# Gate-up product of the experts: 384-column steps that meet the rows' high and low part at once, and a 128-row down product

## What is computed

```python
# x: 4096 tokens x 512; CAP = 192 slots per expert, TOP_K = 8, INTER = 192
xb  = rows of x that each expert got                      # (48, 192, 512)
gu  = jnp.einsum('ech,eoh->eco', xb, gate_up_proj)        # (48, 192, 384)
g, u = jnp.split(gu, 2, axis=-1)
h   = jax.nn.silu(g) * u                                  # (48, 192, 192)
out = jnp.einsum('eci,ehi->ech', h, down_proj)            # (48, 192, 512)
final = zeros.at[tok].add(y * w[:, None])                 # y: rows of out, w: routing weights
```

## Time and profile before

| | |
|---|---|
| median of 3 runs | 1123.43 us (1120.83 to 1123.87) |
| the profiled execution | 1120.8 us |
| its span, first to last instruction | 1119.1 us |
| mean granted TensorE clock | 0.963 |
| busy: TensorE, weight loads | 1040.8 us (93%), 820.0 us (73%) |
| busy: VectorE, ScalarE, GpSimd | 872.7 (78%), 626.7 (56%), 551.8 us (49%) |
| chain that ended last | DMA 25%, TensorE 25%, issue 19%, GpSimd 13%, VectorE 11% |

### The profile page before, as it was taken

One profiled execution on the slowest core, in us unless ns is written; L12 is line 12 of the kernel. 1 busy time (PEld: TensorE's weight loads), 2 busy tenths in 40 slices (PEclk: granted clock), 3 DMA queues, 4 the chain that ended last, 5 costly groups with the idle time before them and its releaser, 6 DMA issues.

```text
span 1119.1 us, 24715 instructions
## 1 busy us (share of the span) xinstructions
PE 1040.8 (93%) x6474; PEld 820.0 (73%) x6474; DVE 872.7 (78%) x2429; ACT 626.7 (56%) x1751; POOL 551.8 (49%) x529
## 2 busy tenths in 40 slices
PE   5998999999999999999999963899999999999992
PEld 4776778878787787878878742777777787778771
DVE  5776888888888888889888753478787787877771
ACT  4554455454555545555455531567676677676761
POOL 2114666666666566666666646124343333333333
PEclk9999999999999999999999975699999999999996
DMA  7999565535231131211212110489999999999973
GB/s 295 364 289 291 201 246 175 183 138 178 72 101 48 47 94 47 92 49 59 82 47 86 39 48 23 147 237 257 242 257 239 250 248 251 244 255 243 255 172 46
DMA packets 94050, 185.70 MB, mean 166 GB/s; under 512 B 24791, under 2 KB 24791, under 8 KB 93504
## 3 DMA queue, kind: packets, MB, share of 16 engines
q1 hardware_dynamic: 62640, 145.10, 40.3%
q0 software_dynamic: 31376, 40.20, 16.5%
HBM read 116.00 MB, written 122.00 MB: 213 GB/s over the span
## 4 chain that ended last, share of the span: by engine, by line
DMA 25%; PE 25%; issue 19%; POOL 13%; DVE 11%; ACT 3%; POOLq 1%; DVEq 1%; SPq 0%; ACTq 0%
DMA layer_out<-qk_both,scatter_idx 21%; PE ps L1180 11%; POOL slot_records L541 6%; PE ps L1165 5%; POOL layer_out L622 4%; DVE qk_both L998 3%; POOL rstd L552 3%; PE ps L1170 2%; PE ps L1298 2%; DMA x_ln<-in_x 2%; DVE diff L993 1%; PE ps L1319 1%; PE ps L1202 1%; DMA slot_records<-row,slot_idx 1%; DMA w_raw<-slot_records 1%
## 5 line engine op out<-in xcount | busy, mean ns | idle before, releaser
L541 POOL DMA_INDIRECT slot_records<-row,slot_idx x256 | 266.4, 1041 | 89.7 <-issue 59.6
L622 POOL DMA_INDIRECT layer_out<-qk_both,scatter_idx x96 | 143.5, 1495 | 262.3 <-DVE scatter_idx L1099 206.2
L552 POOL TENSOR_TENSOR rstd<-mv,neg_half 128x1 f32<-128x1 f32 x96 | 80.2, 835 | 130.4 <-DVE mv L911 78.8
L1180 PE MATMUL ps<-w_high,xn_high 128*128 128x512 f32 x384 | 114.0, 419 | 0.7 <-ACT xn_high L637 0.7
L672 ACT ACTIVATE probs<-ps,neg_max_s 128x128 f32<-128x128 f32 x256 | 89.9, 377 | 33.2 <-DVE neg_max_s L908 33.2
L1180 PE MATMUL ps<-w_low,xn_high 128*128 128x512 f32 x384 | 107.8, 403 | 0.0
L1180 PE MATMUL ps<-w_high,xn_low 128*128 128x512 f32 x384 | 107.0, 401 | 0.0
L637 ACT ACTIVATE xn_t<-ps 128x512 f32<-128x512 f32 x64 | 38.3, 599 | 117.4 <-PE ps L1165 117.4
L1319 PE MATMUL ps<-w_high 128*128 128x192 f32 x576 | 94.1, 286 | 3.6 <-DVE w_low L1085 3.3
L1319 PE MATMUL ps<-w_low,w_high 128*128 128x192 f32 x576 | 89.8, 279 | 0.0
L1319 PE MATMUL ps<-w_high,w_low 128*128 128x192 f32 x576 | 89.6, 278 | 0.0
(11 more groups left out here) (162 smaller groups left out, 2407.6 us busy)
## 6 DMA issues: line engine op xcount, KB each, us to landing
gu_sb<-in_gate_up SPq DMA_DIRECT2D x48, 768.0 KB, 5.4
slot_records<-dn_both SPq DMA_DIRECT2D x6, 3366.0 KB, 23.0
w_raw<-slot_records SPq DMA_DIRECT2D x48, 280.5 KB, 4.7
dn_both<-in_down_proj SPq DMA_DIRECT2D x48, 256.0 KB
x_ln<-in_x SPq DMA_DIRECT2D x32, 256.0 KB
x_res<-in_x SPq DMA_DIRECT2D x32, 256.0 KB, 3.0
ctx_t_sb<-in_ctx_t SPq DMA_DIRECT2D x32, 256.0 KB
ctx_sb<-in_ctx_rows SPq DMA_DIRECT2D x32, 256.0 KB
```

The source lines that it names most:

```text
L541: pool.indirect_dma_start(out=records, out_offset=bass.IndirectOffsetOnAxis(ap=slot_idx[:, s.parity, k:k + 1], axis=0), in_=row[:, s.parit ...
L552: pool.tensor_tensor(rstd[:, :], mv[:, 1:2], neg_half[:, 0:1], ALU.pow).then_inc(steps.sem, 1)
L622: pool.indirect_dma_start(out=out, out_offset=bass.IndirectOffsetOnAxis(ap=scatter_idx[0:PART[h], d.parity, h:h + 1], axis=0), in_=y[0:PAR ...
L1180: last = pe.matmul(dst, left[:, c, :], right[:, m, c, :], start=(n == 0 and c == 0), stop=(n == 2 and c == KC - 1))
```

## The change

The parts of the rows come to lie beside each other (`rows_both`, 2 x 192 columns), and a step of the gate-up product with the weights' high part takes both, 384 columns, into one bank: columns 0 to 191 collect high x high, columns 192 to 383 high x low. The 4 steps with the weights' low part add low x high to the second half. A block now has 8 matmuls instead of 12 and fills its own bank (2, 3 and 6). The two halves are added outside TensorE: ScalarE copies the second half to SBUF (`gu_part`: blocks 0 and 1 in one copy, block 2 in another), VectorE adds the first half to it (`gu_sum`: one addition for blocks 0 and 1, two for block 2, which bring the up part from partitions 64 to 127 down to 0 to 63), and silu and the products h1 and h2 read `gu_sum`. `gu_part` and `gu_sum` lie over the attention's `v_sb` and `probs`.

In the down product the last step takes all 128 rows of `h2_rest`, whose upper half is set to zero once, in place of 64.

```diff
@@ split_buffers
-        gu_high, rows_high, dn_high, dn2_both, h1_high, h2_twice = split_buffers(w_high)
-        gu_low, rows_low, dn_low, _, h1_low, h2_rest = split_buffers(w_low)
+        gu_high, rows_both, dn_high, dn2_both = split_buffers(
+            w_high, (2, KC, 2 * INTER), (2, KC, 2 * CAP), (2, 1, DM), (2, 1, DM))
...
+        rows_high, rows_low = rows_both[:, :, :, 0:CAP], rows_both[:, :, :, CAP:2 * CAP]
@@ ScalarE, expert_turn
                     act.wait_ge(gup_t.sem, gup_t.after(u, "first"))
                     if u.back(1).exists():
-                        act.wait_ge(gup_v.sem, gup_v.after(u.back(1), "h2"))
-                    act.activation(silu1[:, :], ps[:, 2, 0:CAP], ACT.Silu).then_inc(gup_a.sem, 1)
+                        act.wait_ge(gup_v.sem, gup_v.after(u.back(1), "sum2"))
+                    copy(gu_part[:, 0:2, :], ps[:, 2:4, CAP:2 * CAP], gup_a)
                     act.wait_ge(gup_t.sem, gup_t.after(u, "second"))
-                    act.activation(silu2[:, :], ps[0:INTER - P, 3, 0:CAP], ACT.Silu).then_inc(gup_a.sem, 1)
+                    copy(gu_part[:, 2, :], ps[:, 6, CAP:2 * CAP], gup_a)
+                    act.wait_ge(gup_v.sem, gup_v.after(u, "sum1"))
+                    act.activation(silu1[:, :], gu_sum[:, 0, :], ACT.Silu).then_inc(gup_a.sem, 1)
+                    act.wait_ge(gup_v.sem, gup_v.after(u, "sum2"))
+                    act.activation(silu2[:, :], gu_sum[0:INTER - P, 2, :], ACT.Silu).then_inc(gup_a.sem, 1)
@@ VectorE, expert_turn
                 if u.exists():
+                    dve.wait_ge(gup_a.sem, gup_a.after(u, "part1"))
+                    if u.back(1).exists():
+                        dve.wait_ge(gup_v.sem, gup_v.after(u.back(1), "h2"))
+                        dve.wait_ge(gup_a.sem, gup_a.after(u.back(1), "silu2"))
+                    dve.tensor_tensor(gu_sum[:, 0:2, :], ps[:, 2:4, 0:CAP], gu_part[:, 0:2, :], ALU.add)\
+                        .then_inc(gup_v.sem, 1)
+                    dve.wait_ge(gup_a.sem, gup_a.after(u, "part2"))
+                    dve.tensor_tensor(gu_sum[0:INTER - P, 2, :], ps[0:INTER - P, 6, 0:CAP], gu_part[0:INTER - P, 2, :],
+                                      ALU.add)
+                    dve.tensor_tensor(gu_sum[0:INTER - P, 3, :], ps[INTER - P:P, 6, 0:CAP], gu_part[INTER - P:P, 2, :],
+                                      ALU.add).then_inc(gup_v.sem, 1)
...
-                    dve.tensor_tensor(h1[:, :], silu1[:, :], ps[:, 2, CAP:2 * CAP], ALU.mult).then_inc(gup_v.sem, 1)
+                    dve.tensor_tensor(h1[:, :], silu1[:, :], gu_sum[:, 1, :], ALU.mult).then_inc(gup_v.sem, 1)
                     dve.wait_ge(gup_a.sem, gup_a.after(u, "silu2"))
-                    dve.tensor_tensor(h2[:, :], silu2[:, :], ps[INTER - P:P, 3, 0:CAP], ALU.mult)\
+                    dve.tensor_tensor(h2[:, :], silu2[:, :], gu_sum[0:INTER - P, 3, :], ALU.mult)\
...
+                    if u.first():
+                        dve.memset(h2_rest[INTER - P:P].bitcast(FP32), 0.0)
@@ TensorE, expert_turn
                     if u.back(1).exists():
-                        pe.wait_ge(gup_v.sem, gup_v.after(u.back(1), "h2"))
+                        pe.wait_ge(gup_v.sem, gup_v.after(u.back(1), "sum2"))
...
-                        pairs = [(gu_high, rows_high), (gu_high, rows_low), (gu_low, rows_high)]
-                        for n, (left, right) in enumerate(pairs):
-                            for k in range(KC):
-                                last = pe.matmul(dst, left[:, u.parity, k, cols], right[:, u.parity, k, :],
-                                                 start=(n == 0 and k == 0), stop=(n == 2 and k == KC - 1))
+                        for k in range(KC):
+                            pe.matmul(bank[:, 0:2 * CAP], gu_high[:, u.parity, k, cols], rows_both[:, u.parity, k, :],
+                                      start=(k == 0), stop=False)
+                        for k in range(KC):
+                            last = pe.matmul(bank[:, CAP:2 * CAP], gu_low[:, u.parity, k, cols],
+                                             rows_high[:, u.parity, k, :], start=False, stop=(k == KC - 1))
...
-                                 (h2_twice, dn2_both, P), (h2_low, dn2_both, INTER - P)]
+                                 (h2_twice, dn2_both, P), (h2_rest, dn2_both, P)]
```

More of the change, by code:

```diff
@@ L310, in decoder_layer @@
         gup_t = Steps(sem("gate_up_tensor"), "first second")
-        gup_a = Steps(sem("gate_up_scalar"), "silu1 silu2 high1 high2 again")
-        gup_v = Steps(sem("gate_up_vector"), "h1 h2 low1 low2")
+        gup_a = Steps(sem("gate_up_scalar"), "part1 part2 silu1 silu2 high1 high2 again")
+        gup_v = Steps(sem("gate_up_vector"), "sum1 sum2 h1 h2 low1 low2")
         wgu_a = Steps(sem("gate_up_weights_scalar"), "high")
```

18 lines of the change are left out of this document (11 added, 7 removed).

## The result

| | before | changed |
|---|---|---|
| median | 1123.65 us (4 runs, 1120.83 to 1124.88) | 1141.30 us (4 runs, 1140.45 to 1143.16) |
| the profiled execution, its span | 1120.8, 1119.1 us | 1143.16, 1141.4 us |
| one turn of the loop, mean of 43 | 8.09 us | 8.59 us |

The changed kernel takes 1.0154 times as long, 95% interval 1.0116 to 1.0192: slower by 17.6 us. The forecast was slower by 5.6, at 1129; 1141.3 lies near the upper end of its range. The sign and the mechanism held; a part of the mechanism was sized far too small.

A forecast was written before the change was run, and what follows sets the result against it. Three loops near 8 us bound the expert stage; the lengthened ring makes the period 8.30: 43 turns +8.6, first turns 0, end -1.5, together +7, so 1128, and 1129 us against the runs' median. Range 1114 to 1143.

The forecast's parts named there:

- Three loops near 8 us: Expert stage: TensorE's work, the scatter-adds, and a ring of ScalarE and VectorE all close at nearly 8 us.
- the scatters' loop: GpSimd issues an expert's two scatter-adds only after the previous expert's have landed; claimed 8.0 to 8.1 us beside the loads.
- TensorE's turn 8.0 to 6.9: TensorE's work per expert falls from 8.0 to about 6.9 us: 0.6 saved in gate-up, 0.5 in the down product.
- The gaps of 0.32 and 0.43: Down product: start distances around its 64-row step, 0.75 us together; as a 128-row step it saves 0.29.
- ScalarE's copies cost nothing: ScalarE's two copies out of PSUM are covered by VectorE's gu_low (1.76 us); without that cover up to 0.87 per turn.
- The ring at 8.17: Loop from gu_low through index, sums, silu2 and ScalarE's copies to the next gu_high, lengthened from about 6.8 to 8.17 us.
- The lower end: Ring 0.23 us shorter if the gaps at two joints around the third sum and h1 are absent.
- The index's wait ... I take 0.13, near the lower end.: VectorE's index waiting for a scatter landing adds 0 to 0.4 us per turn, taken as 0.13: period 8.30.
- First turns 0, tail -1.5: Half-clock first turns: TensorE's gain cancels the added sums, 0; the end: scatters hang less far behind, -1.5 us.
- Faster: Rival: the ring does not close, so TensorE's gain shows; at best 1107 us, chance 0.14.
- No change, the scatters set the pace: Rival: scatters set the pace as before, or the shorter end pays; 0 to +3 us, 1121 to 1126, chance 0.22.
- Clock: Rival: TensorE's pauses of about 1.2 us lower its clock in the loop; +4.2 us per such turn, chance 0.03.

The follow-up runs named there:

- experiment 11: Kernel before, with SyncE starting the next gate-up load at the end of VectorE's turn, down weights and rows behind it: 1118.5 us, ratio 0.9962.
- experiment 9: Changed kernel, with SyncE starting the next gate-up load at the end of VectorE's turn, down weights and rows behind it: 1128.5 us, ratio 1.0053.
- experiment 5: Changed kernel without ScalarE's two part copies and VectorE's three sums, TensorE's work kept as changed: 1125.3 us, ratio 1.0006.
- experiment 1: Changed kernel, with VectorE making the scatter index just before y1 instead of between gu_low and the sums: 1133.6 us, ratio 1.0084.

## Why the prediction was right in direction and short in size

- **Three loops near 8 us.** Right, and the most useful part. What I missed is that the scatters' loop was closed in nearly every turn: before, the scatters follow each landing by a steady 1.5 us. The chain of waits by line says it in one row (64.8% in the scatters' DMA), and I had read it only for its first turns. TensorE's loop is close behind: in the new order (experiment 11) most turns are its 8.00 and 8.03.
- **TensorE's turn 8.0 to 6.9.** Right: 0.18 and 0.11 us per step, 85% busy in a turn of 8.6 is 7.3, part of it at a lower clock; in experiment 9, at full clock, 85% of 8.24 is 7.0. The gaps of 0.32 and 0.43 are gone. Worth nothing in the loop, as forecast (experiment 5). The Trainium skill's figure for the step, 163 ns from "TensorE: Matmul & The Clock Gate", section Back-to-back issue gap, was a little low: 0.73 / 4 = 0.18 was measured.
- **ScalarE's copies cost nothing.** Right: 848.59 to 849.66, under gu_low, and ScalarE then sits idle 2.48 us before silu1.
- **The ring at 8.17.** Right within 0.07: in experiment 9, where the index never waits, most turns are 8.12 or 8.24 and some up to 8.56, with a mean of 8.24; 8.06 and 8.18 alternate in experiment 1, whose ring lacks the index's 0.07. Its joints as well: first sum 1.75 after gu_low's start (forecast 1.74), second 2.21 (2.21), third 2.57 (2.60), silu2 to row copies 0.27 (0.26). The lower end, 0.23 for gaps that might not be there, did not come. VectorE's own work came out a little smaller than the 7.7 to 7.8 forecast: 88.3% of 8.59 is 7.6, 90.8% of 8.24 in experiment 9 is 7.5.
- **"The index's wait ... I take 0.13, near the lower end."** This is the step that failed, and its size was wrong as well as its reason. Without its waits the changed kernel turns in 8.24 (experiment 9), with them in 8.59: 0.35 us per turn, close to the upper of my ends, or 43 x 0.35 = 15 us where 43 x 0.13 = 5.6 was counted. The recorded waits say nearly the same: 7.8 us in 41 turns, and 0.25 more behind each of the 19, make 0.31 per turn. The reason given was wrong: "the scatters catch up until they are in time", with a loop that "ran at 8.0 to 8.1 beside the loads". I took the scatters' 6.6 us as a constant. It depends on the load work that falls in front of them and beside them, and the gate-up load is released by gu_low, hence by the ring. In the longer turn the scatters come earlier, on average 2.59 us after gu_low's start instead of 3.74, and so 0.3 us ahead of the load's first packet, where before they came 0.8 us behind it. Catching up lengthens them: 0.7 us more of load work stands before their landing. They can't fall back far either, since the index's wait stops that. Not shown is how much of this is the gate-up load's and how much the rows', which moved with it.
- **First turns 0, tail -1.5.** Right in the main: gu_low of the fifth turn starts at 737.34 against 734.50, 2.8 later, of which 2.3 came from the attention stage of that execution and 0.5 from here; the tail is 34.9 against 36.8, -1.9. With 43 x 0.50 = 21.4 this is the 22.3 between the two spans; the before profile was the lowest of its runs and the changed one the highest, so the medians are only 17.6 apart. The split of the first turns held too: without the sums the first four are 5.7 us shorter than before (experiment 5), with them 0.5 longer.
- **The range.** Its ends were not worked out as the forecast was. By the forecast's own sum a period of 8.6 gives 1140.8 us for the profiled execution (43 x 0.5 - 1.5) and 1143.4 for the median, a period of 8.0 gives 1115.0 and 1117.6. The measured 1141.3 is inside either way.
- **Rivals.** *Faster* drew on the rule of the Trainium skill ("Perfetto Trace Analysis", Identifying the Most-Contended Engine) to optimize the most contended engine first, and took TensorE for it by its 99.3% in rows 1. The runs speak against relieving TensorE first here, since experiment 5 does just that and gains nothing. Against the page they say less: it calls TensorE's matmul share no good measure of how close it is to its limit and looks at the share of the weight loads, and by rows 1 that is 77.7%, level with VectorE's 78.7%, the engine that the change loads further. *No change, the scatters set the pace* had the right loop but took its pace as given. *Clock*: it did dip, see below; at 0.98 in the loop it is a small part of the 17.6 us.
- **The signs.** Of the marks of being right, VectorE over 90% busy was missed (88.3%, since the turn got longer). One of the marks of being wrong came true, a granted clock under 1.00, though not as a cause of note. I listed "index still waits 1 us while ScalarE has idle time" as the mark of scatters that bind. The scatters do bind, yet the index waits only 0.2 us on average. A wait at one engine measures its phase, not whether the loop behind it is closed; the distance from landing to the next issue does.

## What to carry to other kernels

A loop with slack on every engine can still be closed through a DMA: look at whether each transfer is issued a fixed time after the last one landed, before pricing any engine. The duration of such a transfer is no constant; it depends on the loads that move when it is issued (6.5 to 7.2 us here), so an edit that moves the release of a load is an edit of the transfer. When two loops lock into a phase, try the order of the loads before you shorten an engine's turn: SyncE's order alone was worth 12.8 us in the changed kernel and 4.7 in the one before, and the wrong order cost that one 21.8. Price an order by running both kernels in it, or its gain is booked to the change.

## What the runs showed of the hardware

Loads in front delay a scatter-add's first data from 2.1 us after the issue to as much as 5.2, although they stand in different queues. In the changed kernel the landing follows the loads' work up to it closely (correlation 0.96 over 38 experts).

Removing a wait can cost time: the late index made the kernel before 0.8% slower and, with a short ring, led to a stable state of 11 us per turn in which nothing was over 75% busy.

The granted clock dipped in the loop of the changed kernel's profile, for short stretches from 787 and from 855 us. Busy time in a stretch of 5 us, then TensorE in order of time there, after an idle 1.97 us:
```profile
854.00:859.00 5.00, 4.20 (x18) 4.20 (x19) 4.55 (x10) 3.95 (x8) 1.39 (x1) 0.66 0.85 201
```
```profile
854.80 1.12 PE L1339 MATMUL ps<-w_high 128*128 128x384 f32 x4 [1.97 <-DVE w_high L1094]
...
856.52 1.53 PE L1339 MATMUL ps<-w_high 128*128 128x384 f32 x4
857.85 1.00 PE L1342 MATMUL ps<-w_high,w_low 128*128 128x192 f32 x4
```
Four 384-column matmuls take 1.33 us (856.52 to 857.85), 0.33 each, at 1.2 GHz, where they take 0.73 at 2.4 GHz. I had given pauses of this size no effect. It cost little, since the loop seldom waits for TensorE: the turn around it took 9.09 us, where other turns whose index waited took 8.8 to 9.5.
